# Six-block decoder on one core: squares of keys and queries move from GpSimd to ScalarE, and the causal mask goes into the banks ahead of the narrow scores

## The reference, cut to what matters

```python
# block 1: attention, 16 heads of 64, not causal ("wide", self)
# block 2: cross attention on the context, 16 heads of 64, one null key and value
q, k = l2_normalize(q_heads) * q_scale, l2_normalize(k_heads) * k_scale    # sum of squares of q and of k
p = softmax(SCALE * q @ concat(null_k, k).T); out = p @ concat(null_v, v)
# block 3: pre-normed causal attention, 16 heads of 8 ("narrow"), then a mixture of 8 experts, top 2
att = einsum('bhqd,bhkd->bhqk', q, k) / sqrt(8)
att = softmax(where(tril, att, -inf)); y = att @ v
# block 4: causal attention over the batch axis; block 5: gated product with the context; block 6: ternary FFN
```

## Time and profile before

| | us |
|---|---|
| median of 3 runs | 697.87 (696.43 to 698.28) |
| the profiled execution | 697.76 |
| its span in the profile | 696.0 |
| mean granted clock of TensorE | 0.986 of 2.4 GHz |

### The profile page before, as it was taken

The page is one execution under the profiler, slowest core; times in us unless marked ns, Lnnn a source line. Parts: engine busy times, 40 slices in busy tenths (PEclk is TensorE's granted clock), DMA queues, the critical chain, the costliest instruction groups (busy, mean ns, idle before and its releaser), DMA issues.

```text
span 696.0 us, 11930 instructions
## 1 busy us (share of the span) xinstructions
PE 647.4 (93%) x4216; PEld 439.0 (63%) x4216; DVE 463.0 (67%) x1298; ACT 380.3 (55%) x1099; POOL 192.9 (28%) x231
## 2 busy tenths in 40 slices
PE   7999999999999999879986879899999999999996
PEld 4676776766767667657663656665767677745543
DVE  2978786875898988988985568684324363584502
ACT  4766566666566766646762466676344345343311
POOL 1221111365565756855134034100000000100101
PEclk9999999999999999999997999999999999999999
DMA  9300000000000000000000000930000000000000
GB/s 283 104 1 1 2 1 1 2 1 1 0 1 2 1 1 1 1 1 2 1 1 1 0 1 2 323 130 1 1 1 0 2 1 1 0 1 0 16 0 15
DMA packets 12729, 15.78 MB, mean 23 GB/s; under 512 B 2168, under 2 KB 9216, under 8 KB 12288
## 3 DMA queue, kind: packets, MB, share of 16 engines
q1 hardware_dynamic: 12384, 14.88, 6.5%
q10 hardware_dynamic: 288, 0.16, 0.1%
HBM read 14.51 MB, written 0.52 MB: 22 GB/s over the span
## 4 chain that ended last, share of the span: by engine, by line
PE 72%; DVE 18%; ACT 6%; issue 2%; POOL 1%; DMA 0%; POOLq 0%; DVEq 0%; SPq 0%; ACTq 0%
PE ring L839 8%; PE ptb L850 8%; PE obank L943 7%; PE ring L916 7%; PE ptb L931 6%; PE ring L868 5%; PE obank L951 4%; PE misc L986 3%; DVE arena L1339 3%; ACT arena L640 3%; PE misc L896 3%; DVE arena L1322 3%; PE misc L897 2%; PE ring L858 2%; PE ring L750 2%; PE ptb L703 2%
## 5 line engine op out<-in xcount | busy, mean ns | idle before, releaser
L640 ACT ACTIVATE arena<-ring,arena 128x256 f32<-128x256 f32 x256 | 129.0, 519 | 5.3 <-DVE arena L1322 5.2
L1339 DVE TENSOR_SCALAR arena<-arena 128x256 f32<-128x256 f32 x256 | 90.7, 399 | 0.0
L1322 DVE TENSOR_REDUCE arena<-ring 128x4 f32<-128x1024 f32 x56 | 68.3, 1220 | 28.6 <-PE ring L916 28.5
L1298 DVE COPY arena<-ptb 128x512 f32<-128x512 f32 x128 | 81.9, 681 | 0.0
L943 PE MATMUL obank<-arena 128*64 128x256 f32 x512 | 72.1, 404 | 3.9 <-ACT arena L616 3.9
L916 PE MATMUL ring<-arena 64*128 64x256 f32 x512 | 73.5, 406 | 0.8 <-ACT arena L640 0.6
L931 PE MATMUL ptb<-ident,arena 128*128 128x128 f32 x512 | 67.8, 276 | 3.2 <-DVE arena L1298 1.8
L578 ACT ACTIVATE arena<-ring,arena 128x512 f32<-128x512 f32 x64 | 42.4, 688 | 49.7 <-PE ring L839 48.5
L931 PEld LDWEIGHTS ptb<-ident,arena 128*128 128x128 f32 x512 | 59.4, 142 | 7.3 <-issue 2.3
L850 PEld LDWEIGHTS ptb<-arena 128*128 128x128 f32 x512 | 59.1, 192 | 3.9 <-issue 3.3
L850 PE MATMUL ptb<-arena 128*128 128x128 f32 x512 | 60.0, 275 | 0.0
(11 more groups left out here) (242 smaller groups left out, 1147.7 us busy)
## 6 DMA issues: line engine op xcount, KB each, us to landing
arena<-in_M_w_dram SPq DMA_DIRECT2D x16, 256.0 KB, 3.8
arena<-in_F_h_dram SPq DMA_DIRECT2D x2, 1024.0 KB, 7.9
arena<-in_B_wkv_dram SPq DMA_DIRECT2D x1, 1024.0 KB, 9.8
arena<-in_F_w_dram SPq DMA_DIRECT2D x3, 256.0 KB, 5.4
rows<-in_rows_dram SPq DMA_DIRECT2D x1, 612.0 KB, 8.5
arena<-in_A_wv_dram SPq DMA_DIRECT2D x1, 512.0 KB, 5.9
x_res<-in_x_dram SPq DMA_DIRECT2D x1, 512.0 KB, 8.5
ctx_tok<-in_ctx_dram SPq DMA_DIRECT2D x1, 512.0 KB, 9.6
```

What stands on the lines that cost most here:

```text
L640: ins = nc.scalar.activation(probs[g % 4][:, c, h, :], ring[:, ring_at["S", g, h] % RING, c * S:(c + 1) * S], ACT.Exp, bias=negmax[:, i, q ...
L1298: nc.vector.tensor_copy(probsT[g % 2][:, :, :, c * P:(c + 1) * P].rearrange("p h k q -> p (h k) q"), ptb[:, c, :].rearrange("p (k q) -> p ...
L1322: ins = nc.vector.tensor_reduce(dst[:, i1, q1, :, :].rearrange("p c h -> p h c"), ring[:, r:r + 2, :].rearrange("p h (c k) -> p h c k", c= ...
L1339: ins = nc.vector.tensor_scalar(a, a, rsum[:, i, q, k // 2, k % 2:k % 2 + 1], None, ALU.mult)
```

## The change

ACT squares each part of keys and queries itself, out of the PSUM bank and ahead of its copy, with the waits that POOL had had; POOL's 32 squares go. DVE's key sums stay in the steps in which they were. In narrow attention `causal` grows to 384 columns (mask, zeros, mask), the product with the identity writes the whole of a bank first (`start=True`) and the scores are added onto it. The masks of banks 2 and 3 stand ahead of the scores in their step, those of banks 0 and 1 in the step before, ahead of the third transpose tile. `c_ring_done` now rises with the second part of the scores of each bank.

```diff
--- before.py
+++ after.py
@@ -111,7 +111,7 @@
         C_wq, C_wk, C_wv, C_wp = [sb("C_w" + n, [P, D]) for n in "qkvp"]
         M_gw, M_b2 = sb("M_gw", [P, E]), sb("M_b2", [E, D])
         hmask, gmask = sb("hmask", [P, H]), sb("gmask", [P, H // 4])
-        causal, identb = sb("causal", [P, P], BF16), sb("identb", [P, P], BF16)
+        causal, identb = sb("causal", [P, P + S], BF16), sb("identb", [P, P], BF16)
         half = const[:, 0, :]
 
         def col(name, i=0, lo=0, hi=P):
@@ -650,11 +650,20 @@
                         if kind == "K":
                             if b >= 3 and r == 0:
                                 act.wait_ge(misc_done, misc_at["pair", PAIRS * (B + b - 2) - 1] + 1)
+                            if r >= 2 or b >= 1:
+                                act.wait_ge(ksum_part, 4 * b + r - 1)
+                            else:
+                                act.wait_ge(null_ready, 1)
+                            nc.scalar.activation(ksq[:, r % 2, :, :].rearrange("p h a -> p (h a)"), src, ACT.Square).then_inc(ksq_ready, 1)
                             nc.scalar.copy(ktok[b % 3][:, c, hf * 512:(hf + 1) * 512], src).then_inc(ring_free, 1)
                         elif kind == "Q":
                             if b >= 2 and r == 0:
                                 act.wait_ge(ring_done, ring_at["S", PAIRS * (B + b - 1) - 1, 1] + 1)
-                            nc.scalar.copy(qT_all[b % 2][:, 2 * r:2 * r + 2, :], src.rearrange("p (a s) -> p a s", a=2)).then_inc(ring_free, 1)
+                            if b >= 1 and r == 0:
+                                act.wait_ge(misc_done, misc_at["sq", b - 1, 0] + 1)
+                            src = src.rearrange("p (a s) -> p a s", a=2)
+                            nc.scalar.activation(qsq[:, 2 * r:2 * r + 2, :], src, ACT.Square).then_inc(qsq_ready, 1)
+                            nc.scalar.copy(qT_all[b % 2][:, 2 * r:2 * r + 2, :], src).then_inc(ring_free, 1)
                     if s >= OVER:
                         null_weights(s)
                     if s - C_AT >= FIRST:
@@ -702,6 +711,11 @@
                         r, lo = (k, 0) if u == 0 else (2 * (u - 1) + k // 2, P + k % 2 * P)
                         ins = nc.tensor.transpose(ptb[:, n % 2, k * P:(k + 1) * P], pr[:, g % PR, r, lo:lo + P], ident[:, :])
                     ins.then_inc(c_pt_done, 1)
+
+                def mask(g, r):
+                    if g >= 1:
+                        pe.wait_ge(c_ring_free, G * (g - 1) + r + 1)
+                    nc.tensor.matmul(ring[:, r, 0:SW], identb[:, :], causal[:, :], start=True, stop=False, skip_group_check=True)
 
                 def narrow_extra(e, s):
                     kind, b = e
@@ -742,17 +756,15 @@
                         pe.wait_ge(kz_pool, 2 * b + q // 2 + 1)
                         if s == 0:
                             pe.wait_ge(ring_free, len(ring_at))
+                        for r in range(0 if s == 0 else 2, G):
+                            mask(s, r)
                         for c, cols_c in enumerate((slice(0, P), slice(P, SW))):
                             for r in range(G):
-                                if s >= 1 and c == 0:
-                                    pe.wait_ge(c_ring_free, G * (s - 1) + r + 1)
                                 lanes = slice(RG * r, RG * (r + 1))
-                                nc.tensor.matmul(ring[:, r, cols_c], qTc[lanes, b % 2, c * P:(c + 1) * P], kzn[lanes, b % 2, q, 0:(c + 1) * P],
-                                                 start=c == 0, stop=c == 1, skip_group_check=True)
-                        for r in range(G):
-                            nc.tensor.matmul(ring[:, r, :].rearrange("p (x k) -> p x k", k=P)[:, 0:3:2, :], identb[:, :],
-                                             causal[:, :].unsqueeze(1).broadcast_to([P, 2, P]), start=False, stop=True,
-                                             skip_group_check=True).then_inc(c_ring_done, 1)
+                                ins = nc.tensor.matmul(ring[:, r, cols_c], qTc[lanes, b % 2, c * P:(c + 1) * P], kzn[lanes, b % 2, q, 0:(c + 1) * P],
+                                                       start=False, stop=True, skip_group_check=True)
+                                if c:
+                                    ins.then_inc(c_ring_done, 1)
                     for e in c_first[s]:
                         narrow_extra(e, s)
                     if CT < s <= NGR + CT:
@@ -783,6 +795,9 @@
                         narrow_tiles(s - CT, 1)
                     for e in c_then[s]:
                         narrow_extra(e, s)
+                    if 0 <= s < NGR - 1:
+                        mask(s + 1, 0)
+                        mask(s + 1, 1)
                     if CT <= s < NGR + CT:
                         narrow_tiles(s - CT, 2)
 
@@ -1458,8 +1473,9 @@
                 ch.step(nc.gpsimd.tensor_tensor(gmask[:, :], gmask[:, :], hmask[:, 3 * G:4 * G], ALU.add))
 
                 ch.step(nc.gpsimd.memset(causal[:, :], 0.0))
-                nc.gpsimd.affine_select(out=causal[:, :], in_=causal[:, :], compare_op=ALU.is_ge, fill=MASKED,
-                                        base=0, pattern=[[-1, P]], channel_multiplier=1)
+                for k in (0, 2):
+                    nc.gpsimd.affine_select(out=causal[:, k * P:(k + 1) * P], in_=causal[:, k * P:(k + 1) * P], compare_op=ALU.is_ge, fill=MASKED,
+                                            base=0, pattern=[[-1, P]], channel_multiplier=1)
                 nc.gpsimd.tensor_copy(identb[:, :], ident[:, :])
                 lns = 0
                 c_ch = Chain(pool, c_pool_steps)
@@ -1510,21 +1526,6 @@
                     return n
 
                 for s in range(STEPS):
-                    for e in ring_extras.get(s - 1, []):
-                        kind, b, r = e
-                        pool.wait_ge(ring_free, ring_at[e] + 1)
-                        if kind == "K":
-                            if r >= 2 or b >= 1:
-                                pool.wait_ge(ksum_part, 4 * b + r - 1)
-                            else:
-                                pool.wait_ge(null_ready, 1)
-                            k2 = ktok[b % 3][:, r // 2, (r % 2) * 512:(r % 2 + 1) * 512].rearrange("p (h a) -> p h a", a=A)
-                            nc.gpsimd.tensor_tensor(ksq[:, r % 2, :, :], k2, k2, ALU.mult).then_inc(ksq_ready, 1)
-                        else:
-                            if b >= 1 and r == 0:
-                                pool.wait_ge(misc_done, misc_at["sq", b - 1, 0] + 1)
-                            q2 = qT_all[b % 2][:, 2 * r:2 * r + 2, :]
-                            nc.gpsimd.tensor_tensor(qsq[:, 2 * r:2 * r + 2, :], q2, q2, ALU.mult).then_inc(qsq_ready, 1)
                     for e in misc_extras.get(s - 1, []):
                         kind, b, r = e
                         if kind == "sqT":
```

## The result

The changed kernel takes 737.24 us (median of 4 runs, 734.51 to 737.76) against 697.15 for the kernel before: ratio 1.057, 95% interval 1.0534 to 1.0605, 40.1 us slower. The forecast was 732 us, between 717 and 746. The profiled execution took 737.76 us with a span of 736.0 and a mean granted clock of 0.961.

A forecast was written before the change was run, and what follows sets the result against it. PE's program order was taken to set the pace, with DVE close behind in cross attention. Stalls +30.1, clock +10.5, POOL relief -6 and masks 0 gave +34.6 us on 697.76: 732 us, range 717 to 746.

The forecast's parts named there:

- part 1: Attention steps: ACT's key squares wait for DVE's sums, so PE stands for `obank` eight times; +30.1 us, bounds 27.6 and 33.
- part 2: Behind the new stalls TensorE's clock falls, costing 1.5 us for seven of the eight; +10.5 us, bounds 0 and 16.
- part 3: The other 24 squares on ACT, 14 us of work ahead of the `obank` copies, are covered and cost nothing.
- part 4: 32 squares leave POOL, so DVE is held less in cross attention; -6 us, between 0 and -11.5.
- The estimate of 27 us: Gain if DVE and POOL's exclusive port lock is taken alone: some 32 x 0.85 = 27 us; the forecast allowed less.
- the cap from PE's idle time: Only DVE delay reaching PE counts: 9.5 us idle from 200 to 320 us, plus some 2 for the clock.
- part 5: Narrow attention: the new masks leave the 16 steps as long as before; 0 us, bounds -6 and +4.
- rival 1: The stalls come but TensorE's clock holds: 722 us, chance 0.22.
- rival 2: Upper ends of stalls and clock, with no relief for DVE: 747 us, chance 0.08.
- rival 3: About half of the stalls are absorbed, by DVE and ACT running ahead or shorter second waits: 712 us, chance 0.13.
- rival 4: Cross attention: DVE's port is the bound and the wait is covered, so faster, up to 688 us; chance 0.04.
- rival 5: Square on ACT needs its own table, two loads around each of 32 squares: 82 us, over 800 in all; chance 0.03.

The follow-up runs named there:

- c2_four_slots: The changed kernel with four slots for the key squares in place of two, key sums where they were: 692.28 us, ratio 0.9911 to the kernel before.
- experiment 9: Kernel before with only query squares on ACT, plus an unused same-size POOL product at the same 16 places: 697.73 us, ratio 1.0016.
- experiments 3 to 5: Against the kernel before: squares on ACT with old masks, 737.37 us; new masks alone, 697.01 us; squares on ACT with four key slots and old masks, 691.07 us.
- c6_pe_kept_busy: Changed kernel, but PE computes the next K or Q part three more times before its `obank` wait in eight steps: 720.56 us, ratio 1.0335.

## Why the prediction was right

**The stalls (part 1), right in place, number and size.** The working gave 3.05 us for each of the self steps; the trace has 2.94, 3.09 and 3.21. For the five cross steps I took 4.2 and gave 3.7 and 4.8 as ends; they are 3.78, 3.89, 4.09, 3.89 and 4.09. The sum was put at 30.1 us and is 29.0. The upper end of 4.8 had taken all of DVE's lateness in one step as part of the wait: 5.29 us from the scores to the end of the sum. After the change two such steps have 4.48 and 4.70 us (L931 at 237.31 and 307.03, sum's end at 241.79 and 311.73), so DVE does catch up in part, as the part said. Square took 597 ns, between the bounds.

**The clock (part 2), right in kind and mis-sized.** The term was +10.5 us, from 1.5 us each for seven stalls; it measures 16.7 us, 2.1 each for eight. The step that failed is the length at half clock: I took the loss within a single window of 3 us from the earlier trace rows as the whole of it, when the window at 381 us was at half clock to its end. Behind the first stall PE ran slow from 125.78 to 132.20, 6.42 us for what takes 3.40 at full clock (L943 at 123.74 to the next L916 at 127.14). That is 3.0 us lost, twice what I took, though behind other stalls it was as little as 1.6. That an eighth stall would be spared was wrong as well. The measured term lies at the upper bound of 16 us, and that bound rested on 4 us at half clock, which no row gave. The term's excess of 6.2 us is more than the 5 us by which the forecast was low; the stalls, 1.1 below their term, took some of it back.

**The other 24 squares (part 3), right at nothing.** c2_four_slots has all 32 squares on ACT and is faster than before.

**POOL's squares (part 4), right: -6 us was taken.** The gain without stalls is 5.6 us with the masks and 5.3 without them, and 4.3 for the query squares alone. That DVE is held by POOL's product had rested on one pair of rows; experiment 9 shows that this product makes the difference. The estimate of 27 us, every product counted in full, would have been far off; the cap from PE's idle time was the right reading, but that the middle was so close is luck, as nothing had been worked out inside the bounds of 0 and 11.5. That the K squares would be worth none of it was not separated beforehand. DVE's products of 4 elements a row were to stay under 0.4 us except beside POOL's scaling of the keys (L1557): six are longer after the change, five beside that scaling and one, of 0.59 us, beside a POOL product of a layernorm.

**The masks (part 5), right at 0.** DVE's first minimum in the step shown comes 1.52 us after the masks of banks 2 and 3 begin (463.70 - 462.18), where 1.34 was expected, and the stage is 0.4 us shorter between the two marks. The last mask is held a little by ACT's exponentials of the step before (the row at 462.43, 0.26 us), which let its bank go only then: ACT's exponentials lie in the same chain, so a shorter PE part there would have been taken back by them. That reading of the balance is argued from the rows of one step; what the runs show is that the new masks change nothing that can be measured (experiments 3 to 5).

**The rivals.** 722 us with the clock holding (rival 1) is what c6_pe_kept_busy built, at 720.56; the changed kernel did not go that way. Upper ends everywhere and no relief (rival 2) did not come together: the clock reached its upper end, the stalls did not, and the relief was there. No stall was absorbed (rival 3): the second of each batch is as long as the first or longer. Nothing was covered (rival 4). The faster kernel that this rival described does exist, though, once the wait is gone: c2_four_slots, at 692.28. No table load stands at a square (rival 5); the changed kernel has as many loads as before.

Sum with the measured terms: 29.0 + 16.7 - 5.6 = 40.1 us, which is the measured difference. As 16.7 and 5.6 are themselves differences of these kernels, this tests one thing only: that the 29.0 us counted in the trace are what the stalls cost, for which the runs by themselves give 28.3.

## What to carry to other kernels

When work moves to another engine, its waits move with it, and what they cost is set by what is queued behind them there: a wait that costs POOL nothing costs PE 3 to 4 us when ACT takes it, because ACT's next copy is what PE stands for. Before moving, look for the wait in the list of waits of the old engine and give it room: two more buffers of 128x512 turned a kernel 5.7% slower than before into one 0.9% faster. Here room was better than order: the same sums one step earlier ran into the next wait in the chain.

## What was not expected of the hardware

- A stall of 2.94 us on a TensorE that had been busy costs more than itself: some 6 us at 1.2 GHz followed (125.78 to 132.20). The loss was not the same behind every stall, from 1.6 to 3.2 us by the windows, and 2.1 us on average by experiment 6, where I had put it at 1.5. Work without use in the gap won back 16.7 us.
- A POOL product that is no part of the computation, at 16 places of 1.04 to 1.12 us, cost a kernel 6.0 us (697.73 against 691.71), or 4.7 between runs with the same mean clock. DVE products of 0.15 us beside it took up to 1.00.
